# Four layers of attention and experts on one core: the exact scores of layer 0 and of the rotary layer multiplied in four strips of 32 weight columns

## What is computed

```python
# layer 0
q = shape(x @ Wq + bq); k = shape(x @ Wk + bk); v = shape(x @ Wv + bv)     # (4, 16, 1024, 8)
scores = einsum('bhqd,bhkd->bhqk', q * scale, k) + position_bias * 8.0
attn = softmax(scores, axis=-1)
ctx_out = einsum('bhqk,bhkd->bhqd', attn, v)
...
# rotary layer
q = q * cos + rotate_half(q) * sin;  k = k * cos + rotate_half(k) * sin
scores = einsum('bhqd,bhkd->bhqk', q, k) / sqrt(HD)
attn = softmax(scores, axis=-1)
ao = einsum('bhqk,bhkd->bhqd', attn, v)
```

## Time and profile before

| | |
|---|---|
| median of 3 runs | 5675.41 us (5665.6 to 5683.95) |
| the profiled execution, its own time | 5673.37 us |
| its span, first to last instruction | 5671.6 us (1.8 us lie around it) |
| mean granted TensorE clock | 0.949 of full speed |
| PE busy | 5233.6 us, 92% of the span |
| DVE busy | 3977.0 us, 70% |
| ACT busy | 2753.7 us, 49% |
| layer 0, about 80 to 950 us of the span | 870 us |
| rotary layer, about 2600 to 3359 us | 759 us |

### The profile page before, as it was taken

The page is one execution under the profiler, slowest core; times in us unless marked ns, Lnnn a source line. Parts: engine busy times, 40 slices in busy tenths (PEclk is TensorE's granted clock), DMA queues, the critical chain, the costliest instruction groups (busy, mean ns, idle before and its releaser), DMA issues. The chain is left out here.

```text
span 5671.6 us, 86273 instructions
## 1 busy us (share of the span) xinstructions
PE 5233.6 (92%) x31277; PEld 2622.8 (46%) x31277; DVE 3977.0 (70%) x6826; ACT 2753.7 (49%) x4661; POOL 1338.7 (24%) x933
## 2 busy tenths in 40 slices
PE   6999998787999999999999979899999999997999
PEld 2333332444567777773222228533433434335676
DVE  7888886774577677777888953678788787864322
ACT  4766666321233333335776866455454454452333
POOL 0120100230112322322112213244444443440000
PEclk7999999787999999999999989999999999998999
DMA  4211110002111111111111212100000000001000
GB/s 89 47 32 31 32 31 11 0 0 62 37 34 24 30 26 29 28 28 31 26 38 35 43 47 80 40 15 18 12 13 20 12 13 12 12 13 38 5 5 8
DMA packets 148359, 156.96 MB, mean 28 GB/s; under 512 B 48980, under 2 KB 95108, under 8 KB 147508
## 3 DMA queue, kind: packets, MB, share of 16 engines
q1 hardware_dynamic: 143336, 142.37, 11.6%
q0 software_dynamic: 4096, 8.40, 0.5%
q10 hardware_dynamic: 504, 0.69, 0.1%
HBM read 118.20 MB, written 37.40 MB: 27 GB/s over the span
## 5 line engine op out<-in xcount | busy, mean ns | idle before, releaser
L4091 DVE TENSOR_REDUCE wide_max_parts<-wide_p 128x2 f32<-128x1024 f32 x496 | 595.3, 1220 | 128.9 <-PE wide_p L4060 113.2
L790 ACT ACTIVATE attn_w<-l_p 128x512 f32<-128x512 f32 x1024 | 549.3, 597 | 238.8 <-DVE l_p L1236 131.8
L2589 PE MATMUL caus_p<-caus_x_one,big 128*128 128x129 f32 x4608 | 641.8, 286 | 0.0
L641 DVE TENSOR_REDUCE l_max_parts<-l_p 128x2 f32<-128x1024 f32 x512 | 602.3, 1219 | 50.2 <-PE l_p L617 45.2
L641 DVE TENSOR_REDUCE rot_max_parts<-rot_p 128x2 f32<-128x1024 f32 x488 | 574.3, 1219 | 64.3 <-PE rot_p L617 62.2
L2673 ACT ACTIVATE big<-caus_p 128x512 f32<-128x512 f32 (+3 forms) x768 | 345.6, 489 | 553.2 <-PE caus_p L2575 402.2
L2589 PEld LDWEIGHTS caus_p<-caus_x_one,big 128*128 128x128 f32 x4608 | 592.5, 199 | 36.3 <-issue 3.0
L4368 PE MATMUL wide_p<-arena 64*128 64x512 f32 x2048 | 529.5, 596 | 0.0
L4506 ACT ACTIVATE attn_w<-wide_p 128x1024 f32<-128x1024 f32 x342 | 350.1, 1024 | 333.3 <-PE wide_p L4368 331.4
L4299 POOL TENSOR_TENSOR big<-big,attn_w 128x1024 f32<-128x1024 f32 x128 | 333.3, 2604 | 392.9 <-PE wide_p L4060 380.9
L641 DVE TENSOR_REDUCE caus_max_parts<-caus_p 128x2 f32<-128x1024 f32 (+2 forms) x360 | 340.5, 956 | 24.2 <-PE caus_p L617 15.9
(11 more groups left out here) (645 smaller groups left out, 8952.5 us busy)
## 6 DMA issues: line engine op xcount, KB each, us to landing
arena<-q_parts SPq DMA_DIRECT2D x576, 32.0 KB
arena<-k_parts SPq DMA_DIRECT2D x576, 32.0 KB
arena<-inverse_rows SPq DMA_DIRECT2D x64, 256.0 KB
l_q_stack<-q_parts SPq DMA_DIRECT2D x279, 32.0 KB
l_k_stack<-k_parts SPq DMA_DIRECT2D x279, 32.0 KB
q_parts<-arena SPq DMA_DIRECT2D x8, 768.0 KB, 3.6
k_parts<-arena SPq DMA_DIRECT2D x8, 768.0 KB, 3.6
attn_w<-moe_in SPq DMA_DIRECT2D x19, 256.0 KB
```

What stands on the lines that cost most here:

```text
L641: self.nc.vector.tensor_reduce(self.max_parts[:, 2 * p:2 * p + 2, n, half], pair[:, :, 0:self.width(n, half)], AX.X, ALU.max).then_inc(*se ...
L790: self.nc.scalar.activation(self.exps[t % len(self.exps)], bank, ACT.Exp).then_inc(*self.exped.up())
L2589: mm = nc.tensor.matmul(outs[o % 2][:, nq % 2 * (C + 1):(nq % 2 + 1) * (C + 1)], exps[h % 2][:, kb, nq * P:(nq + 1) * P], x_one[b % 2][:, ...
L4091: self.nc.vector.tensor_reduce(self.max_parts[:, :, n, h], side, AX.X, ALU.max).then_inc(*self.maxed.up())
```

## The change

The weight columns of an exact score (128 keys) are cut into four strips of 32. Each strip is a matmul of its own with the same moving operand, and writes its own 32 partitions of the bank. The near bias is cut in the same way. Nothing else changes: the same products go to the same places, and only the last of the matmuls increments the semaphore.

```diff
-        mm = nc.tensor.matmul(bank, heads.k_stack[i][0:STACK, j, kb * P:(kb + 1) * P],
-                              heads.q_stack[i][0:STACK, j, half * BANK:(half + 1) * BANK], start=True,
-                              stop=near is None)
+        strips = [slice(self.W * m, self.W * (m + 1)) for m in range(P // self.W)]
+        for strip in strips:
+            mm = nc.tensor.matmul(bank[strip, :],
+                                  heads.k_stack[i][0:STACK, j, kb * P + strip.start:kb * P + strip.stop],
+                                  heads.q_stack[i][0:STACK, j, half * BANK:(half + 1) * BANK], start=True,
+                                  stop=near is None)
         if near is not None:
...
             for s in range(SPLITS):
-                mm = nc.tensor.matmul(bank[:, lo - half * BANK:hi - half * BANK], core.flip_bf[:, :],
-                                      bias[:, s, first + j, lo - kb * P:hi - kb * P], start=False,
-                                      stop=s == SPLITS - 1)
+                for strip in strips:
+                    mm = nc.tensor.matmul(bank[strip, lo - half * BANK:hi - half * BANK],
+                                          core.flip_bf[:, strip],
+                                          bias[:, s, first + j, lo - kb * P:hi - kb * P], start=False,
+                                          stop=s == SPLITS - 1)
         mm.then_inc(*heads.scored.up())
```

## The result

The changed kernel takes 5630.65 us (median of 4 runs, 5626.77 to 5640.33) against 5676.34 for the kernel before on the same chip: a ratio of 0.9929, 95% interval 0.9917 to 0.9941. The forecast was 5667 us, with a range from 5647 to 5710, and missed it: the gain is 46 us where 8 were forecast. The profiled execution has a span of 5625.0 us.

What follows compares the result with a forecast made beforehand. PE was taken to bound both layers, DVE close behind. Rotary 10 us less and layer 0 2 us more made 8 us less than the profiled 5673.4, so 5665; the median, 2 us above, gave 5667, range 5647 to 5710.

Steps and rivals of the forecast that it cites:

- What bounds the kernel; changes of shape at 0.09 to 0.10: Layer 0 and rotary layer: PE bounds both, DVE close behind; each change of tile shape on PE leaves 0.09 to 0.10 us.
- the first load of a strip shape costs 0.03 where the full shape cost 0.01: Exact scores in strips on PE: first weight load behind a shape change takes 0.03 us, against 0.01 for the full shape.
- leaving exact scores for another shape costs 0.02 more: PE, exact scores to another tile shape: strips start some 7 ns apart, so leaving them costs 0.02 us more.
- part of it falling into waits of PE: Layer 0, 103 groups with an inserted step: 15 us more if whole, part absorbed by PE's waits, 13 taken.
- half of the 0.20 is lost to DVE's loop: Plain rotary groups: PE saves 0.20 us each, the wait for DVE's maxima takes half; 142 x 0.10 = 14 us less.
- 15 us less if whole, 7 if halved; I take 11: Layer 0, some 150 plain groups: one shape change fewer, 0.10 us each, perhaps halved by waits; 11 us less taken.
- the 10 groups without maxima unchanged (ACT's four exponentials): Rotary layer, 10 groups without maxima: ACT's four exponentials named as the reason for no change in time, 0 us.
- the whole gain arrives: Rival, 20%: PE's whole gain arrives; rotary layer 24 us less, layer 0 even, total 5651 us.
- shape does not decide: Rival, 12%: 0.09 us stays between bf16 score and f32 weighing despite equal tile shapes; strips cost some 13 us, total 5688.
- Slow instructions: Rival, 7%: PE's instructions come too slowly, deciding from 31 ns each; at 57 ns the total is about 6220 us.
- Loads one after another: Rival, 7%: the strips' weight loads run one after another, 0.11 us a round, not hidden behind near bias; 5730 to 5760.
- bf16 strips: Rival, 4%: bf16 strips do not stream side by side on PE, 0.88 us for 0.22; 1350 us more, about 7020.

## Why the prediction was wrong

Its mechanism stands: fewer changes of shape shorten PE's order, and DVE's loop holds a part of it back. Its sum was too small in five terms of six for the two layers, which all erred to the same side, most of all in the groups with inserted steps (some 18 us of the difference). Summed over groups, from one weighing to the next, in the two profiles of each kernel:

| term | forecast, us | measured, us |
|---|---|---|
| rotary, plain groups | -14 | -14 to -15 |
| rotary, inserted steps | +4 | -6 to -7 |
| rotary, no maxima | 0 | -2 |
| layer 0, plain groups | -11 | -16 to -17 |
| layer 0, inserted steps | +13 | +4 to +6 |
| layer 0, no maxima | 0 | -2 |
| the rest of the program | 0 | -12 and -3 |

- **What bounds the kernel; changes of shape at 0.09 to 0.10**: right. 0.09 to 0.10 in the timelines, 0.11 from the 576 changes of the near bias in one piece, the weighing's 0.03 included.
- **"the first load of a strip shape costs 0.03 where the full shape cost 0.01", and "leaving exact scores for another shape costs 0.02 more"**: the step that failed. I took both from the weighing, which stands behind a change of shape, and charged them to the exact scores in strips. Behind exact scores of the same shape the weighing runs without that 0.03 (1.03 us instead of 1.06), and the exact strips don't pay it in its place: a transpose is followed by them 0.08 later than by a full exact score, which is the change of shape alone, and maxima to exact score keeps its 0.53. Nor does leaving them cost more: exact score to maxima keeps its 0.53 too. So PE's own gain in a plain rotary group is 0.23, not 0.20, and an inserted transpose, four changes before and four after, costs 0.02 less than before (3.09 to 3.07 us), not 0.04 more. In layer 0 an inserted step costs 0.04 to 0.09 more in most groups, not 0.15. On some 100 such groups a layer that is 6 us in the rotary layer and about 8 in layer 0, most of what these two terms were off by.
- **"part of it falling into waits of PE"** was said for layer 0 and then hardly counted. Behind a projection (L367) the fourth exact score already waited for its bank, which ACT had to free; part of the new time went into that wait, and those groups got 0.13 shorter in the rotary layer (medians 3.71 and 3.58).
- **"half of the 0.20 is lost to DVE's loop"**: right in kind, shown by the runs with half the maxima. In size the term came out (143 plain groups give 14 to 15 us together, 0.10 each, of 0.23), but partly by luck: the plain groups under 2.95 us went from 2.62 to 2.55 us on average, so the loop takes two thirds of the 0.23 there, and 3 to 4 us of the 14 to 15 come from the few longer groups, of which there are fewer.
- **"15 us less if whole, 7 if halved; I take 11"** in layer 0: whole was right. A plain group with near bias lost 0.13 (3.28 to 3.15 us), with half the maxima just as much. Such a group takes 3.15 us, against 2.36 for its two reductions; the rotary loop was carried over to a layer most of whose groups are too long for it.
- **"the 10 groups without maxima unchanged (ACT's four exponentials)"**: wrong. They went from 2.40 to 2.18 us, so PE's order bound them and not ACT.
- **Near bias at nothing**: right; even a gain, since near bias to weighing no longer changes shape.
- **The rivals.** That the whole gain arrives (5651) was nearest by number, by luck: it had 24 us in the rotary layer with plain groups at their whole 0.20, while of the 22 to 23 measured there the plain groups gave 14 to 15, at half; and layer 0, "even" there, brought 12 to 15. That shape does not decide falls by the two strips of 64. Slow instructions fall: 7 ns for one in the near bias, where it would have decided from 31 on, and twelve near matmuls pass in 0.17 us. The Trainium skill (TensorE: Matmul & The Clock Gate, on the 56 ns gap) has some 62 ns of microcode for a matmul where hardware decode is off; by that, the twelve would need an estimated 0.75, which the trace does not show. (The prediction's "some 190 us more" by the same figure should have been some 215.) Loads one after another fall by the same row. The Trainium skill (TensorEngine Tiling (Array Packing), Restrictions and Gotchas) excludes Fast Weight Load for column tiles, but no wait of the strips for their loads shows beside the matmuls. bf16 strips do run side by side: eight in 0.61 us.
- **The range** ended at 5647, the whole-gain rival with layer 0 even. No case had both layers gain, although the costs of all inserted steps hung on one reading and would fall together. The 12 us outside the two layers in the first pair of profiles were in no case either, though the range would have missed without them too: 34 us of the 46 are left, where the range ended at a gain of 28.

## What to carry to other kernels

On a TensorE-bound stretch, list the tile shapes in PE's order and count the neighbours that differ: each such pair costs 0.09 to 0.11 us here, the busy times don't show it, and splitting a matmul's columns into four strips of its neighbour's shape costs next to nothing (into two of 64 it cost 0.02 for two scores). All operations of one run of steps must be cut alike (the near bias left whole cost 63 to 66 us), and the next step to cut is the one that now stands between two equals. When an overhead is read from one row, ask what stands in front of that row, because the change may move just that.

## What was unexpected of the hardware

- The 0.03 us that I had put to the first weight load is no fixed cost of a tile of 32 columns: it is there behind another shape (1.06 us for eight weighing records) and gone behind the same shape (1.03), although data type and rows differ (bf16 of 98 rows, then f32 of 128). Exact scores of 32 columns behind another shape don't show it.
- Cutting two exact scores into eight bf16 strips costs 0.01 us (0.61 for 0.60), less than the weighing's f32 strips had led me to think.
- An untouched layer took 961 us in one kernel and 967 to 970 in another, at mean granted clocks of 0.95 and 0.94, and a second profile of each kernel did not make the difference go away. It belongs to the measured gain, but no cost of the changed instructions holds it.
